# Bonus sums of a recurrent block in four column groups, with one product that spreads them

## The reference

```python
def step(s, rkvw):
    r_t, k_t, v_t, w_t = rkvw
    a = k_t[..., :, None] * v_t[..., None, :]
    out = jnp.einsum('bhi,bhij->bhj', r_t, u * a + s)
    s = a + w_t[..., :, None] * s
    return (s, out)
```

## Time and profile before

| | |
|---|---|
| three timed runs | 951.91 to 957.22 us, median 955.3 us |
| the profiled execution | 953.33 us |
| its span, first to last instruction | 951.6 us |
| granted TensorE clock, mean | 0.965 of 2.4 GHz |
| busy: PE / DVE / POOL / ACT | 92% / 72% / 56% / 41% |

### The profile page before, as it was taken

One profiled execution on the slowest core, in us unless ns is written; L12 is line 12 of the kernel. 1 busy time (PEld: TensorE's weight loads), 2 busy tenths in 40 slices (PEclk: granted clock), 3 DMA queues, 4 the chain that ended last, 5 costly groups with the idle time before them and its releaser, 6 DMA issues.

```text
span 951.6 us, 10578 instructions
## 1 busy us (share of the span) xinstructions
PE 877.9 (92%) x3588; PEld 392.8 (41%) x3588; DVE 688.8 (72%) x875; ACT 388.2 (41%) x755; POOL 535.4 (56%) x573
## 2 busy tenths in 40 slices
PE   2789999999989997999899998999979999799988
PEld 1234433443434442444344444444435444444454
DVE  6336799899879996889889999779995324523442
ACT  3032323332234322213235454554446353736394
POOL 1001685888949789399789996888873101010200
PEclk8698999999979998899999999999989999999999
DMA  8082458465773639265734043446002212010101
GB/s 288 11 169 86 122 145 167 143 177 138 155 185 113 186 80 196 70 171 147 208 106 112 24 105 103 109 109 163 17 23 67 78 33 79 0 45 1 44 1 44
DMA packets 93943, 100.34 MB, mean 105 GB/s; under 512 B 22850, under 2 KB 64066, under 8 KB 91842
## 3 DMA queue, kind: packets, MB, share of 16 engines
q1 hardware_dynamic: 86978, 87.09, 36.3%
q10 hardware_dynamic: 6912, 12.59, 3.8%
HBM read 65.05 MB, written 33.55 MB: 104 GB/s over the span
## 4 chain that ended last, share of the span: by engine, by line
PE 54%; DVE 16%; POOL 10%; issue 6%; ACT 5%; DMA 4%; SPq 3%; ACTq 0%; DVEq 0%; POOLq 0%
PE PS L1359 36%; PE PS L1488 3%; DVE M L1072 3%; DVE VB L1188 3%; PE PS L1592 3%; POOL VB L755 3%; PE PS L1368 3%; POOL VB L751 2%; POOL VB L747 2%; PE PS L1426 2%; PE PS L1569 2%; DMA scr_v<-STG 2%; DVE VB L1069 2%; SPq L497 2%; PE PS L1503 1%
## 5 line engine op out<-in xcount | busy, mean ns | idle before, releaser
L1359 PE MATMUL PS<-M,W 128*128 128x512 f32 x544 | 264.4, 628 | 15.5 <-DVE M L1072 11.6
L1359 PEld LDWEIGHTS PS<-M,W 128*128 128x128 f32 x544 | 102.4, 199 | 154.2 <-issue 138.1
L747 POOL TENSOR_TENSOR VB<-KR,VB 128x1008 f32<-128x1008 f32 x64 | 129.8, 2028 | 58.0 <-PE PS L1488 53.3
L1188 DVE TENSOR_TENSOR_SCAN VB<-PS,VB 128x512 f32<-128x512 f32 x128 | 149.0, 1206 | 16.1 <-POOL VB L755 14.2
L755 POOL TENSOR_TENSOR VB<-VB 128x1008 f32<-128x1008 f32 x64 | 151.1, 2362 | 3.5
L1069 DVE TENSOR_TENSOR VB<-VB,PS 128x2048 f32<-128x2048 f32 x64 | 146.0, 2282 | 2.0
L635 POOL TENSOR_SCALAR NM<-MV 128x2 f32<-128x2 f32 (+1 forms) x24 | 5.4, 227 | 231.2 <-DVE MV L1316 141.7
L751 POOL TENSOR_TENSOR VB<-WG,VB 128x1008 f32<-128x1008 f32 x64 | 128.7, 2011 | 0.1
L1359 PE MATMUL PS<-W,M 128*128 128x512 f32 x224 | 105.7, 597 | 0.0
L1334 DVE TENSOR_REDUCE SM<-PS 128x1 f32<-128x512 f32 x64 | 43.4, 687 | 55.7 <-PE PS L1592 55.0
L1488 PE MATMUL PS<-VB,HEAD 128*32 128x512 f32 x512 | 69.7, 617 | 5.2 <-DVE VB L1069 5.0
(11 more groups left out here) (176 smaller groups left out, 1317.8 us busy)
## 6 DMA issues: line engine op xcount, KB each, us to landing
VB<-scr_vs SPq DMA_DIRECT2D x64, 256.0 KB, 7.5
W<-in_w SPq DMA_DIRECT2D x8, 1024.0 KB, 9.2
scr_vs<-STG SPq DMA_DIRECT2D x64, 64.0 KB, 5.1
scr_v<-STG SPq DMA_DIRECT2D x16, 256.0 KB, 6.3
scr_w<-STG ACTq DMA_DIRECT2D x16, 256.0 KB, 5.0
scr_k<-STG ACTq DMA_DIRECT2D x16, 256.0 KB, 2.1
KR<-scr_k SPq DMA_DIRECT2D x16, 256.0 KB, 4.2
WG<-scr_w SPq DMA_DIRECT2D x16, 256.0 KB, 5.6
```

The costliest lines, as they stand in the source:

```text
L747: po.tensor_tensor(vo, KO[:, 0:N2 - 1].unsqueeze(1).to_broadcast([P, S, N2 - 1]), VB[:, 2 + s, 0, :, 1:N2], ALU.mult).then_inc(g_kv, 1)
L1188: sc = dv.tensor_tensor_scan(s_, PS[:, 5, :], b_, 0.0, ALU.mult, ALU.add)
L1359: mm = pe.matmul(o, l, r, start=i == 0, stop=i == 3)
```

## The change

- HEAD and HEADU shrink from 128 x 128 to 128 x 32 per chunk; POOL's three copies that repeated HEAD are gone, and ACT's four scalings write a quarter.
- The bonus sums of a batch are 32 products with 32 columns of weights: for each chunk and each of four column groups g, 32 columns of RQ (with HEADU) and 16 columns (with HEAD). Group g of the time steps lands on partitions 32g to 32g+31, in columns 192 to 239 of PSUM bank 7.
- ACT copies the four groups onto a block diagonal tile DG (128 x 192, elsewhere zero, set once by POOL), times 16. These are four instructions of 32 partitions x 48 columns.
- PE multiplies DG by SAME (which holds 1/16) in one product of 192 columns into bank 7. After that the sums stand on all partitions as before, in groups of 48 columns.
- DVE's two products read them there, with patterns of one more dimension and as many elements as before.
- The counts on p_end rise from three to four a batch, and the waits on it with them. The sums of squares and the norm are unchanged.
- All five lists are in another order. The piece `end` now stands four times a batch in PE's list (bonus, spread, squares, GS) and three times in ACT's. In PE's new list other work stands between bonus and spread in 15 of the 16 batches: one product or attention piece in batches 7 and 11, two pieces in 2, 5, 6 and 10, four or more in 0, 1, 3, 4, 8, 9, 12, 13 and 15; nothing in batch 14 (`end:2` below). In SP's list the store of batch 2's OT moves ahead: before it stood between the third and the fourth of the scattered stores of v for chunk 2 of the third quarter, now it stands ahead of all four; the load of the next quarter's x (1 MB) moves from behind the stores of chunk 3 to ahead of them.

```diff
...
 ORDER_PE = (
...
-    "end:1 c:1 scan:1 l:8 scan:1 l:6 c:1 l:5 c:2 l:1 end:1 l:5 c:1 l:1 c:1 end:1 c:8 l:2 c:4 l:2 c:4 l:5 "
...
+    "scan:1 c:3 end:1 c:11 l:1 scan:1 l:3 c:2 l:4 c:2 scan:1 c:8 l:1 scan:1 l:1 c:4 l:2 end:1 scan:1 "
+    "end:2 l:6 c:3 l:2 c:2 l:1 c:2 l:1 c:4 l:2 c:1 scan:1 l:1 c:2 l:1 c:1 l:1 c:1 end:1 l:11 scan:1 c:8 "
...
 ORDER_SP = (
...
-    "load:1 p:5 x:1 p:10 end:1 p:7 a:1 load:5 end:1 load:1 c:1 load:1 c:1 load:2 a:1 p:2 a:1 load:1 p:1 "
...
+    "load:3 p:11 end:1 p:5 a:1 p:5 load:2 end:1 load:8 c:2 load:1 p:2 a:4 end:1 load:1 p:4 load:1 p:5 "
...
         S0 = sb("S0", [P, B * C4, S])
-        HEAD = sb("HEAD", [P, C4, 4, H])
-        HEADU = sb("HEADU", [P, C4, 4, H])
+        HEAD = sb("HEAD", [P, C4, H])
+        HEADU = sb("HEADU", [P, C4, H])
+        DG = sb("DG", [P, 4, 48])
         SAME = sb("SAME", [P, 4, H])
...
             sem("a_" + n) for n in ("xn", "ext", "xx", "cp", "td", "ex", "gt")]
-        a_s0, a_wr, a_rg, a_end, a_wol = [
-            sem("a_" + n) for n in ("s0", "wr", "rg", "end", "wol")]
+        a_s0, a_wr, a_rg, a_end, a_dg, a_wol = [
+            sem("a_" + n) for n in ("s0", "wr", "rg", "end", "dg", "wol")]
         a_aff, a_xnc, a_exc, a_rl, a_kk, a_rr = [sem("a_" + n) for n in ("aff", "xnc", "exc", "rl", "kk", "rr")]
...
                     if bb >= 2:
-                        w.wait_ge(p_end, 3 * bb - 4)
+                        w.wait_ge(p_end, 4 * bb - 5)
                     sp.dma_start(KR[:, s, 1], of_batch("r", bb)).then_inc(d_rg[s], 16)
...
                     yield
-                for g in range(1, 4):
-                    w.wait_ge(v_hd, C4)
-                    po.tensor_copy(HEAD[:, :, g], HEAD[:, :, 0]).then_inc(g_sel, 1)
-                    yield
                 yield
-                w.wait_ge(g_sel, 10)
+                w.wait_ge(g_sel, 7)
                 po.affine_select(out=MASK[:], in_=MASK[:], compare_op=ALU.is_ge, fill=0.0, base=0,
                 yield
-                w.wait_ge(g_sel, 11)
+                w.wait_ge(g_sel, 8)
                 po.affine_select(out=MASK[:], in_=MASK[:], compare_op=ALU.is_ge, fill=0.0, base=H - 1,
                                  pattern=[[H, 4], [0, H]], channel_multiplier=-1).then_inc(g_sel, 1)
+                yield
+                po.memset(DG[:], 0.0).then_inc(g_sel, 1)
                 yield
...
                     yield from newton(GR[:], GV[:], GT[:], g_end, 14 * bb)
-                    w.wait_ge(p_end, 3 * bb)
+                    w.wait_ge(p_end, 4 * bb)
                     w.wait_ge(v_wm, 5)
                     w.wait_ge(g_end, 14 * bb + 13)
-                    w.wait_ge(g_sel, 12)
+                    w.wait_ge(g_sel, 9)
                     po.tensor_tensor(GS[:], GR[:].unsqueeze(1).to_broadcast([P, 4, H]), MASK[:], ALU.mult).then_inc(g_end, 1)
...
             def stream_end():
-                w.wait_ge(g_sel, 9)
+                w.wait_ge(v_hd, C4)
                 w.wait_ge(d_wl, 64)
                 for m in range(C4):
-                    ac.activation(flat(HEADU[:, m]), flat(HEAD[:, m]), ACT.Copy, scale=U[:, m:m + 1]).then_inc(a_end, 1)
+                    ac.activation(HEADU[:, m], HEAD[:, m], ACT.Copy, scale=U[:, m:m + 1]).then_inc(a_end, 1)
                 yield
                 for bb in range(B):
+                    w.wait_ge(p_end, 4 * bb + 1)
+                    w.wait_ge(g_sel, 10)
+                    for g in range(4):
+                        rows = slice(H * g, H * g + H)
+                        ac.activation(DG[rows, g], PS[rows, 7, 192:240], ACT.Copy, scale=float(S)).then_inc(a_dg, 1)
+                    yield
                     w.wait_ge(v_ot, 5 * bb + 4)
-                    w.wait_ge(p_end, 3 * bb + 1)
+                    w.wait_ge(p_end, 4 * bb + 2)
                     w.wait_ge(a_rg, bb + 1)
                     yield
-                    w.wait_ge(p_end, 3 * bb + 2)
+                    w.wait_ge(p_end, 4 * bb + 3)
                     w.wait_ge(g_end, 14 * bb)
...
                             w.wait_ge(v_kr2, 3 * B)
-                            w.wait_ge(p_end, 3 * B)
+                            w.wait_ge(p_end, 4 * B)
                         elif ks == 3:
...
                         w.wait_ge(d_kg[s], 16 * (bb // 2 + 1))
-                        w.wait_ge(p_end, 3 * bb - 2 if bb else 0)
+                        w.wait_ge(p_end, 4 * bb - 3 if bb else 0)
                         tt(RQ[:, :, 0:L], R, KR[:, s, 0], ALU.mult).then_inc(v_kr2, 1)
...
                     w.wait_ge(g_sel, 1)
-                    dv.tensor_reduce(HEAD[:, m, 0], ID[:].rearrange("p (g h) -> p h g", h=H), AX_X,
+                    dv.tensor_reduce(HEAD[:, m], ID[:].rearrange("p (g h) -> p h g", h=H), AX_X,
                                      ALU.add).then_inc(v_hd, 1)
...
-                    w.wait_ge(p_end, 3 * bb + 1)
+                    w.wait_ge(p_end, 4 * bb + 2)
                     w.wait_ge(d_v4, 16 * (bb + 1))
                     V = KR[:, bb % 2, 1]
-                    tt(T, V[:, :, EVEN], PS[:, 7, L:L + N2].unsqueeze(1).to_broadcast([P, C4, N2]),
-                       ALU.mult).then_inc(v_ot, 1)
+                    own, odd = [PS[:, 7, 0:192].rearrange("p (g n) -> p g n", g=4)[:, :, part].unsqueeze(1)
+                                for part in (slice(0, 32), slice(32, 48))]
+                    tt(T.rearrange("p c (g n) -> p c g n", g=4), V[:, :, EVEN].rearrange("p c (g n) -> p c g n", g=4),
+                       odd.to_broadcast([P, C4, 4, 16]), ALU.mult).then_inc(v_ot, 1)
                     yield
                     w.wait_ge(d_o, 16 * bb)
-                    tt(OT[:], V, PS[:, 7, 0:L].unsqueeze(1).to_broadcast([P, C4, L]), ALU.mult).then_inc(v_ot, 1)
+                    tt(OT[:].rearrange("p c (g n) -> p c g n", g=4), V.rearrange("p c (g n) -> p c g n", g=4),
+                       own.to_broadcast([P, C4, 4, 32]), ALU.mult).then_inc(v_ot, 1)
                     yield
...
                     yield
-                    w.wait_ge(p_end, 3 * bb + 3)
+                    w.wait_ge(p_end, 4 * bb + 4)
                     tt(OT[:], OT[:], PS[:, 7, 3 * L:4 * L].unsqueeze(1).to_broadcast([P, C4, L]), ALU.mult).then_inc(v_ot, 1)
...
                     for g in range(4):
-                        mm = pe.matmul(PS[32 * g:32 * g + 32, 4, :], HEAD[:, m, 0], VB[:, k % NB, :, 4 * g:4 * g + 4].rearrange("p s j n -> p j s n"),
+                        mm = pe.matmul(PS[32 * g:32 * g + 32, 4, :], HEAD[:, m], VB[:, k % NB, :, 4 * g:4 * g + 4].rearrange("p s j n -> p j s n"),
                                        start=m == 0, stop=m == C4 - 1)
...
                     w.wait_ge(v_mad, 6)
-                    w.wait_ge(g_sel, 9)
+                    w.wait_ge(v_hd, C4)
+                    w.wait_ge(a_end, C4)
                     w.wait_ge(v_ot, 5 * bb)
-                    w.wait_ge(a_end, C4)
-                    for wt, cols in ((HEADU, slice(0, L)), (HEAD, slice(L, L + N2))):
+                    for wt, at, n, to in ((HEADU, 0, 32, 192), (HEAD, L, 16, 224)):
                         for m in range(C4):
-                            mm = pe.matmul(PS[:, 7, cols], flat(wt[:, m]), RQ[:, m, cols], start=m == 0,
-                                           stop=m == C4 - 1)
+                            for g in range(4):
+                                mm = pe.matmul(PS[H * g:H * g + H, 7, to:to + n], wt[:, m],
+                                               RQ[:, m, at + n * g:at + n * g + n], start=m == 0, stop=m == C4 - 1)
                     mm.then_inc(p_end, 1)
+                    yield
+                    w.wait_ge(a_dg, 4 * (bb + 1))
+                    w.wait_ge(g_sel, 6)
+                    pe.matmul(PS[:, 7, 0:192], SAME[:].rearrange("p g h -> p (g h)"), flat(DG[:]), start=True,
+                              stop=True).then_inc(p_end, 1)
                     yield
...
```

## The result

The changed kernel takes 930.54 us (median of 4 runs, 928.47 to 931.52) against 955.33 us before in the same session: ratio 0.974 [0.971, 0.977], a gain of 24.8 us. The forecast was 946.5 us, a gain of 8.8, and the range ended at 933. The sign was right and the size was not. Two more measurements beside other kernels gave 0.974 [0.969, 0.980] and 0.978 [0.974, 0.981].

What follows compares the result with a forecast made beforehand. PE was taken as the engine with least slack; 953.3 - 7.2 (products) + 2.0 (spread wait) - 3.5 (lists) = 944.6 us for the profiled execution, which lies 2.0 below the median, so 946.5 us; range 933 to 963.

Steps and rivals of the forecast that it cites:

- The bonus products: On PE, bonus block and spread take 1.13 us a batch instead of 1.73, saving 9.6 us in 16 batches.
- The floor of small records: Rival: PE's small records take 20 ns each, 1.76 us against 1.73, so no saving and 954 us; chance 0.06.
- Conversion 0.75: Share of saved PE time that shortens the kernel: 9.6 us saved on PE become 7.2.
- The wait for the spread: PE waits at the spread for ACT's copies, mainly in batches 14, 7 and 11: adds 2 us, bounds 0 and 17.6.
- The rival: PE's list at the spread, behind ACT's copies: 1.1 us exposed a batch, 17.6 us, kernel slower at 965.7; chance 0.19.
- ACT's copies: Four PSUM copies at 0.26 us, 1.04 us a batch, 17 us in all, covered by ACT's slack: taken as 0.
- The lists: Reordered engine lists: 3.5 us gained by one priced move, the other moves 0 with some 8 us either way.
- The moved store: SP's store of batch 2's OT ahead of four stores of v: gains 3.5 of 8.3 us, bounds 0 and 8.3.
- the first stall: PE idle 4.17 us near 268 us plus 4.1 us lost to low clock after it: 8.3 us, 3.5 counted.
- the second stall: PE's stall near 376 us, cited only as an example of low clock after a wait; no gain counted.
- The absorbed case: Rival: products shorten but PE waits for the recurrence's loop through POOL and DVE; conversion 0.25, 955 us; chance 0.17.

Runs made afterwards that it cites:

- The experiment in the old lists: The new bonus products, copies and spread put into the old lists of the kernel before: 976.14 us, 1.026 of the kernel before.
- the lists alone: All five new lists with the old bonus products, against the kernel before: 941.91 us (0.990), repeated 939.94 us (0.987).
- The kernel that is new up to step 36: Old products, all five lists new up to about the recurrence's step 36 of 64 and old after, against the kernel before: 945.13 us, 0.993.

## Why the prediction was wrong in size

**The bonus products: right, a little small.** I said 0.80 + 0.33 = 1.13 us against 1.73, and the trace has 1.01. Over all batches it is 11.0 / 16 = 0.69 for the block and 6.4 / 16 = 0.40 for the spread. The saving on PE was 12.7 us where I had 9.6, mostly because the old blocks cost 30.1 us and not 27.7: I took one block at full clock for all 16.

**The floor of small records: refuted.** 32 records go by in 0.28 us (181.69 to 181.97) and 32 in 0.41 with the switch, 9 to 13 ns from one to the next. By the rule of about 25 ns from start to start (the Trainium skill, "TensorE: Matmul & The Clock Gate", section "Wait — 56ns, not 53.3ns?") this block would be 1.6 us, an estimate from the page; the trace disagrees where the records go to four column groups in turn.

**Conversion 0.75: about right in the new lists, zero in the old.** 9.8 of 11.4 us is 0.86. In the sum the products with their wait stood at 7.2 − 2.0 = 5.2 us and measured 9.8, so this term too was too small, by 4.6. And the product half can't be priced apart from the lists: in the old lists the same saving is worth nothing (1.006 against 1.004), and going the other way in the new ones 9.5 us cost 3.0, so one factor for both directions doesn't exist. I gave the factor a reason from the earlier trace rows, shares of a mean, and it says nothing of the order.

**The wait for the spread: right place in kind, wrong engine.** I took 2.0 us on PE, and removing copies and wait altogether gave 1.2. In the trace batch 14 waits 1.07 us, where I had 1.1, and batches 7 and 11, where I had 0.25 to 0.6 each, don't wait. The rival wanted 17.6 us on PE's list. The experiment in the old lists lost 24 us, some 20 of them by that wait, though on DVE's list: I had written that T "comes about 2.5 us later" without harm, as the sums that it meets come tens of us later. That asks only who needs T. The question in the instructions of a strict list is who stands behind T, and that is the scan's product. The new DVE list has T where the spread is done: 4.5 us of waiting in place of 24.6.

**ACT's copies: right.** 12.8 us busy, hidden.

**The lists: the step that failed.** "The other moves can't be priced from rows; 0, with some 8 us either way." The moved store came near in size (3.5, measured 3.0) by luck: I had the wait for it gone, and it only fell from 3.57 to 2.49 us. But the runs show 10 to 13 us for the lists, most of it won in the two places of the earlier trace rows. I had both in view, priced one and left the second, the longest stall of the stretch, at nothing. By the same working it was 6.04 us idle and (1 − 0.62) × 10 = 3.8 us of clock, 9.8 us. With the first stall's 8.3 this makes 18. By the traces of the lists alone, 5.5 to 6.9 us came back at the first stall and 6.4 to 9.3 at the second; in the changed kernel it was 4.2 and 6.7. At the share that I gave the first (3.5 of 8.3, so 7.6 of 18) the sum would have been 953.3 − 7.2 + 2.0 − 7.6 = 940.5 and the forecast 942.5; with both stalls gone it is 932, and the range would have reached the result. Rows of before alone couldn't say that the second stall goes, and moves made one by one show how easily the time isn't won (0.995, 1.000, 1.008).

**The absorbed case** did not come in the changed kernel. It exists: the short products in the old lists, with T later, have 6.1 us less work on PE and 7.2 us more idle time. The kernel that is new up to step 36 loses 6 of its 12 us in the same way, where PE, early, meets a DVE that isn't.

What stays open: which pieces of the new lists, between the stalls, make them work together. No single move gives more than 3 us. Only the kernel without the copies took less time than the changed one, by 1.2 us, which is within the noise, and it leaves the bonus out.

## What to carry to other kernels

Where every engine runs a strict list, price a new wait by what is queued behind the waiting instruction, not by who needs its result; here T and the products behind it, 2.5 us too early, cost 2% of the kernel. Price every stall together with the low clock after it, the longest first, and when all lists are rewritten count a share of each instead of zero. In this kernel a saving on the bounding engine was worth nearly its full size in lists cut for it and nothing in the old ones: measure the edit and the reordering apart before calling either one good.

## What the runs showed of the hardware

- Products of 128 x 32 weights with 16 or 32 columns, going to four column groups in turn, follow each other in 9 to 13 ns, each with a weight load of its own. A product with 128 x 128 weights takes 108 ns a record with 128 columns and with 64; that the weight load sets this price is my reading, no run takes it apart.
- ACT's copy of 32 partitions x 48 columns out of PSUM takes 199 ns, less than the 286 ns of 128 x 32 with a bias; four in a row take 0.86 us, 0.22 each.
- More work on PE didn't lower the granted clock: with the bonus products issued twice its mean over six executions was 0.979, and 0.976 over the six of the changed kernel beside them.
- What a stall of PE cost beyond its own length: between steps 12 and 16, around the idle time of 4.17 us, PE lost 4.9 us to the low clock, and 5.4 between steps 24 and 28, around the one of 6.04.
